# Two MLPs computed from rounded halves in three products instead of in fp32

## What is computed

```python
# layer three (L2)
h = _layer_norm(x, ln_mlp_scale, ln_mlp_offset)
h = jax.nn.gelu(h @ w_fc1 + b_fc1, approximate=False) @ w_fc2 + b_fc2
return x + h
# layer four (L3), after its two attentions
ln_out = layernorm(x, ln3_s, ln3_b)
mlp_out = gelu(ln_out @ w1 + b1) @ w2 + b2
return x + mlp_out
```

## Time and profile before

| | us |
|---|---|
| median of 3 runs | 2345.29 (2340.04 to 2346.04) |
| the profiled execution | 2333.35 |
| its span on the core | 2331.6 |
| TensorE busy | 2082.6 (89%) |
| ScalarE, VectorE, GpSimd busy | 995.9, 944.8, 658.7 |
| mean granted TensorE clock | 0.949 of full speed |
| MLPs of layer three | 1698.7 to 1849.2 |
| attention of layer four | 1849.3 to 2206.1 |
| MLPs of layer four | 2206.1 to 2326.9 |

### The profile page before, as it was taken

One profiled execution on the slowest core, in us unless ns is written; L12 is line 12 of the kernel. 1 busy time (PEld: TensorE's weight loads), 2 busy tenths in 40 slices (PEclk: granted clock), 3 DMA queues, 4 the chain that ended last, 5 costly groups with the idle time before them and its releaser, 6 DMA issues.

```text
span 2331.6 us, 37925 instructions
## 1 busy us (share of the span) xinstructions
PE 2082.6 (89%) x15565; PEld 1649.3 (71%) x15565; DVE 944.8 (41%) x1726; ACT 995.9 (43%) x2601; POOL 658.7 (28%) x768
## 2 busy tenths in 40 slices
PE   7877788887899999999899999999889877878799
PEld 4555566654688888888788888888755555666566
DVE  3433222302454444445454444444311267667510
ACT  3332344351343443434343343434344356666522
POOL 2311212112232231313223132321120156656500
PEclk9987899997999999999999999999989898989899
DMA  4000000001010000000001000000020100000000
GB/s 135 10 6 1 6 1 1 1 1 41 3 44 19 10 28 1 28 1 19 1 19 46 1 28 10 10 1 1 1 83 0 46 1 2 6 1 6 1 19 19
DMA packets 28174, 38.36 MB, mean 16 GB/s; under 512 B 1744, under 2 KB 19808, under 8 KB 28000
## 3 DMA queue, kind: packets, MB, share of 16 engines
q1 hardware_dynamic: 28000, 35.93, 4.8%
HBM read 33.83 MB, written 2.10 MB: 15 GB/s over the span
## 4 chain that ended last, share of the span: by engine, by line
PE 75%; DVE 8%; ACT 8%; issue 3%; POOL 3%; DMA 1%; SPq 0%; DVEq 0%; ACTq 0%; POOLq 0%
PE ps L184 33%; PE ps L2105 6%; PE ps_four L2251 5%; PE ps_four L2271 4%; PE ps_four L2089 4%; PE ps L2089 3%; PE ps_four L2260 2%; ACT l_pt L1472 2%; POOL l_sm L1322 2%; PE ps_four L2019 2%; PE ps L2147 2%; DVE l_sm L1829 2%; PE ps L2281 1%; PE ps L2057 1%; PE ps L2065 1%
## 5 line engine op out<-in xcount | busy, mean ns | idle before, releaser
L1566 ACT ACTIVATE l_prob<-ps_four,l_mx 128x129 f32<-128x129 f32 x512 | 181.3, 367 | 593.5 <-DVE l_mx L1864 593.5
L1356 POOL TENSOR_TENSOR l_prob<-l_prob,l_mx 128x516 f32<-128x516 f32 x128 | 134.1, 1048 | 779.5 <-DVE l_mx L1871 779.5
L184 PE MATMUL ps<-l_hT,l_wq 128*128 128x512 f32 x768 | 210.8, 410 | 6.5 <-DVE l_V L1852 6.5
L184 PE MATMUL ps<-ctxT,l_wk 128*128 128x512 f32 x768 | 214.3, 415 | 0.0
L184 PEld LDWEIGHTS ps<-l_wo,l_ao 128*128 128x128 f32 x1536 | 197.8, 188 | 21.1 <-DVE l_ao L1883 7.0
L184 PE MATMUL ps<-l_wo,l_ao 128*128 128x256 f32 x1536 | 204.9, 283 | 5.5 <-DVE l_ao L1883 5.5
L184 PE MATMUL ps<-l_wv,ctxT 128*128 128x512 f32 x768 | 204.6, 402 | 3.7 <-POOL l_wv L1294 3.4
L1322 POOL TENSOR_TENSOR l_sm<-l_sm,l_mask 128x1024 f32<-128x1024 f32 x64 | 149.9, 2363 | 155.7 <-DVE l_sm L1829 155.7
L184 PEld LDWEIGHTS ps<-l_wv,ctxT 128*128 128x128 f32 x768 | 143.8, 190 | 47.4 <-ACT l_qT L1547 9.0
L1795 DVE TENSOR_TENSOR x_tok<-x_tok,ps 128x512 f32<-128x512 f32 x100 | 64.7, 684 | 274.1 <-PE ps L2105 212.1
L184 PEld LDWEIGHTS ps<-l_hT,l_wq 128*128 128x128 f32 x768 | 135.8, 190 | 30.3 <-issue 7.2
(11 more groups left out here) (230 smaller groups left out, 3797.6 us busy)
## 6 DMA issues: line engine op xcount, KB each, us to landing
l_staging<-in_L_xattn_wv SPq DMA_DIRECT2D x8, 512.0 KB, 3.8
l_staging<-in_L_xattn_wk SPq DMA_DIRECT2D x8, 512.0 KB, 3.9
l_staging<-in_L_xattn_wq SPq DMA_DIRECT2D x8, 512.0 KB, 4.2
l_staging<-in_L_xattn_wo SPq DMA_DIRECT2D x8, 512.0 KB, 3.8
x_tok<-in_x SPq DMA_DIRECT2D x4, 512.0 KB, 7.4
ctx_tok<-in_ctx SPq DMA_DIRECT2D x4, 512.0 KB, 5.8
l_mlp_w<-in_L_xattn_mlp_w SPq DMA_DIRECT2D x2, 1024.0 KB, 8.8
l_w<-in_L_xattn_w_fc SPq DMA_DIRECT2D x2, 1024.0 KB, 6.3
```

What stands on the lines that cost most here:

```text
L184: ins = e.matmul(out, a, b, start=start and i == 0, stop=stop and i == 2, skip_group_check=not check)
L1356: e.tensor_tensor(pr[:, :, 0:S + 1], pr[:, :, 0:S + 1], mx[:, 3, :].unsqueeze(2).to_broadcast([P, GB, S + 1]), ALU.mult).then_inc(sem("poo ...
L1566: ins = e.activation(pr.t[:, b, 0:S + 1], banks[b // 2].t[:, (b % 2) * (S + 2):(b % 2) * (S + 2) + S + 1], ACT.Exp, bias=mx[:, 1, b:b + 1] ...
```

## The change

`mlp_split` takes the place of `mlp32` in both layers (layer two keeps `mlp32`):

- `w1` and `w2` are split in halves by VectorE, each in two pieces of 128 x 1024 (`mlp_w`): for layer three before and during the first MLP, for layer four behind the attention.
- The normalised input of each MLP is split by VectorE, two pieces of 128 x 512 (`mhs`), into a tile that exists once.
- Up and down are `matmul_split`: six instructions of 512 columns, and twelve of 256.
- Gelu is made twice from the bank: once into the high half of the hidden tile (rounded), once back into the bank itself in fp32. VectorE subtracts the first from the second into the low half (`hid3`). The hidden tile exists twice.
- In the code below the first `hid3` is ScalarE's, the second VectorE's, `mhs` is VectorE's and `up3` TensorE's. `down3`, `mlp_w` and `mlp_tiles` are built alike.
- The down product of chunk `k - 2` follows the up product of chunk `k` (before: `k - 1`).
- The tiles of layer four's attention (`l3_sm`, `l3_pt`, `l3_mask2`) share memory with the MLP tiles, before and after them.

```diff
+    def mlp_weights(self, phase, landed):
+        for name in ("w1", "w2"):
+            for part in range(2):
+                self.pl.emit("mlp_w", phase, name, part, landed=landed)
+                yield
+
+    def mlp_input(self, u, m, hs_done):
+        pl = self.pl
+        yield from pl.until(self.mhs)
+        pl.slot(self.mhs, "mhs", m)
+        for c in range(DC):
+            pl.emit("mhs", m, c, src=u, src_done=hs_done)
+            yield
+        pl.free(*u, by=("dve.mhs", m, DC - 1))
+
+    def mlp_split(self, m, phase, b1, func):
...
+        for k in range(FC + 2):
+            if k < FC:
+                yield from pl.until(self.misc)
+                pl.bank(self.misc, "up3", m, k)
+                pl.emit("up3", m, k)
+                yield
+            if k == FC - 1:
+                pl.free("mhs", m, by=("full", "up3", m, k))
...
+            if k >= 2:
+                pl.emit("down3", m, k - 2)
+                pl.free("hid3", m, k - 2, by=("pe.down3", m, k - 2))
+            if k < FC:
+                pl.slot(self.hid3, "hid3", m, k)
+                pl.emit("hid3", m, k)
+                pl.free("up3", m, k)
+            yield
...
         def norm3(g):
             yield from output("b", g, "w_co")
             h_done["l3e", g] = yield from normalised(3, g, "b2")
+            if g >= 2:
+                yield from self.mlp_input(("hs", ("l3n", 3, g)), ("l3e", g), h_done["l3e", g])
...
-        run(norm2(0))
-        interleave(mlp2(0), chain(norm2(1), self.load_weight("l3_w_kv", a["L3_xattn_w_kv"], "pool")), 1.2)
+            first, weights = norm2(0), self.mlp_weights("l2m", ("sp.l2m_plain", 32))
+            for stages, n in ((first, 5), (weights, 2)):
+                for _ in range(n):
+                    next(stages)
+            run(first)
+            interleave(mlp2(0), chain(weights, norm2(1), self.load_weight("l3_w_kv", a["L3_xattn_w_kv"], "pool")), 1.2)
...
-        run(rest)
+        attention.close()
+        probs_done, over_done = ("full", "four", "l3", N - 1, 1), ("full", "over", "l3", N - 1)
+        self.mlp_tiles("l3e", scope, (probs_done, over_done, ("pool.l3_scores", N - 1)))
+        interleave(rest, self.mlp_weights("l3e", ("sp.l3_mlp", 32)), 1.0)
...
+        def hid3(m, k):
+            f, bk, hid = self.mlps[m], use["up3", m, k], use["hid3", m, k]
+            q.wait_ge(*pl.event(("full", "up3", m, k)))
+            q.wait_ge(*pl.event(hid.before))
+            table(f["func"])
+            e.activation(hid.t[:, 0, :], bk.t, f["func"], bias=f["b1"][:, k:k + 1])
+            e.activation(bk.t, bk.t, f["func"], bias=f["b1"][:, k:k + 1]).then_inc(sem("act.hid3"), 1)
...
+        def mhs(m, c):
...
+            e.tensor_copy(hi, src).then_inc(sem("dve.mhs:hi"), 1)
+            q.wait_ge(*pl.done("dve.mhs:hi", m, c))
+            e.tensor_tensor(lo, src, f32(hi), ALU.subtract).then_inc(sem("dve.mhs"), 1)
+
+        def hid3(m, k):
+            bk, hid = use["up3", m, k], use["hid3", m, k].t
+            q.wait_ge(*pl.done("act.hid3", m, k))
+            e.tensor_tensor(hid[:, 1, :], bk.t, f32(hid[:, 0, :]), ALU.subtract).then_inc(bk.slot.empty, 1)
...
+        def up3(m, k):
...
+            q.wait_ge(*pl.done("dve.mlp_w", f["phase"], "w1", 1))
+            q.wait_ge(*pl.done("dve.mhs", m, DC - 1))
+            bk = fill("up3", m, k)
+            for c in range(DC):
+                ins = matmul_split(e, bk.t, [half[:, c, k * P:(k + 1) * P] for half in w], [half[:, c, :] for half in hs],
+                                   c == 0, c == DC - 1)
+            ins.then_inc(bk.slot.full, 1)
```

More of the change, by code:

```diff
@@ L196, in __init__ @@
         self.x_done, self.dma_n = [None] * G, {}
-        self.last_norm, self.slack = {}, 0
+        self.last_norm, self.slack, self.mlp_w = {}, 0, {}
     def sb(self, name, shape, dt=F32, scope=None):
@@ L644, in mlp32 @@
         pl = self.pl
-        self.mlps[m] = dict(hs=hs, hs_done=hs_done, w1=w1, w2=w2, b1=b1, func=func, landed=landed)
+        self.mlps[m] = dict(down="pe.mlp_down", hs=hs, hs_done=hs_done, w1=w1, w2=w2, b1=b1, func=func, landed=landed)
         for k in range(FC + 1):
@@ L1092, in halves, with mlp_halves @@
         return self.pl.use[src].t[:]
+    def mlp_halves(self, phase, name):
+        return [self.mlp_w[phase, name][0][:, i] for i in range(2)]
     def rows_of(self, u, b):
```

86 lines of the change are left out of this document (66 added, 20 removed).

## The result

| | median, us | range | ratio to before, 95% interval |
|---|---|---|---|
| before, beside it | 2338.90 | 2336.24 to 2346.04 (6 runs) | |
| after | 2355.40 | 2350.57 to 2360.48 (6 runs) | 1.0064 [1.0042, 1.0085] |

What follows compares the result with a forecast made beforehand. TensorE was taken as the bound, with 75% of the time. Terms of -35.2, +15.3, +6.8, +2.85, +19.9 and +2.9 summed to +12.5 us; from the runs' median of 2345.29 that gave 2358 us, range 2345 to 2374 (8 in 10).

Steps and rivals of the forecast that it cites:

- a, the products: Up and down products of the MLPs: a chunk falls from 3.44 to 2.89 us, -35.2 us over 64 chunks.
- rival of the cheap product: MLP products at half the fp32 price: 20 us less, minus 7, giving 2338 us; chance 0.04.
- b, the starts: First up products of layers three and four wait for VectorE's rounding of weights and input: +8.3 and +7.0 us.
- c, the tails: At each MLP's end the last down product waits 0.85 us for the last chunk's gelus and subtraction: eight times, +6.8 us.
- d, the seams: Between MLPs the next up product waits for the input's rounding, 0.85 us at four seams: +2.85 us in all.
- e, the transposes: TensorE's waits at the normalisations' transposes beside the MLPs grow, as two downs now stand behind them: +19.9 us, largest term.
- Rival 1: The waits at the transposes don't grow: 2338 us, or 2333 with the clock kept up too; chance 0.13.
- f, the clock: TensorE restarts at half clock after idle time: four at 1.7 us, 6.9 against 4.0 now, +2.9 us (0 to 6).
- Rival 3: VectorE is slower than its medians, all rounding at stretched durations: 2371 us; chance 0.14.

Runs made afterwards that it cites:

- starts: The kernel after, with layer three's first GpSimd bias addition held until the input's halves are made and layer four's w2 rounded later: 2343.11 us, ratio 1.0016 to before.
- three_hid: The kernel after, with a third buffer for the halves of the hidden rows in layer four's MLPs: 2349.64 us, ratio 1.0034 to before.
- transposes_late: The kernel after, with the normalisations' transposes placed later in TensorE's order in layer three's second and third MLP: 2328.22 us, ratio 0.9949 to before.
- after_again: The kernel after, unchanged, run and profiled once more: 2355.38 us, ratio 1.0075 to before.
- after_warm2: The kernel after, with unneeded TensorE products filling its long waits, made to end before the data arrive: 2338.62 us, ratio 1.0007 to before.
- two_behind_only: The kernel before, with only the order changed: down products two chunks behind up products, fp32 products and one gelu kept: 2348.44 us, ratio 1.0031 to before.
- combined_warm: The kernel after with late transposes, changed starts, third layer-four hidden buffer, filler products in three waits, one earlier input rounding: 2313.51 us, ratio 0.9890 to before.

## Why the prediction was right, and where its terms were off

Sign and size were right (+12.5 us forecast, +15, 10 to 20, measured), and the largest loss is the one it named, the waits at the transposes. But its terms were off in both directions and cancelled, and that is luck.

The time came near by luck too. 2358 us is 12 above the sum for the profiled execution, by the 2345.29 of three runs; beside the result the median of before was 2338.90, and from there the same +12.5 us give 2351.4, where 2355.4 was measured.

**a, the products: -39.7 us, not -35.2.** A chunk takes 2.82 us, not 2.89: the up product 1.38 us, not the 1.47 of the earlier trace rows, the down product 1.44 for 1.42. The rival of the cheap product (2.58 to 2.60 us) falls: a product of 512 columns with a weight load before it takes 1.38 / 6 = 230 ns. The Trainium skill ("TensorE: Matmul & The Clock Gate", Back-to-back issue gap) gives 216 ns for an isolated one and some 131 ns in a stream with weight loads; these MLPs are above both. The term was off by a reading of the earlier trace rows: the prediction took the first distance there, 1.47 us (1204.52 to 1205.99), for six products of 512 columns; the next six in the same rows take 1.39 (1205.99 to 1207.38), beside the 1.38 of after. 64 times 0.07 is 4.5 us. Its sentence that TensorE never waits in the MLPs holds for layer three's last MLP, not for all: the earlier trace rows show the waits that term e counts.

**b, the starts: 8.1 and 6.7 us, forecast 8.3 and 7.0.** Right, with its mechanism: starts took GpSimd away and the subtraction fell to 1.23 us, and took w2's copy away and the wait went.

**c, the tails: eight of 0.68 us, forecast 0.85.** The step was right (three_hid). The pair of gelus takes 0.58 + 0.65 = 1.23 us. The row that was missing is there now: 0.65 us with PSUM as the destination (fp32), 0.69 with SBUF (rounded), as for the fp32 tile of the earlier trace rows. The Trainium skill ("ScalarE: Activation LUTs", Step-by-step) calls PSUM the lower-latency one, and this trace agrees, by 0.04 us.

**d, the seams: 1.11 us twice and 0.43 twice, and 1.54 at layer three's end: 4.6 us, less the 0.85 of the earlier trace rows that went, +3.8; forecast +2.85.** Behind layer three's MLPs TensorE waited for the additions to `x_tok` that empty the side banks, which the prediction had not looked at there, not for the input's halves.

**e, the transposes: +17.8 us, forecast +19.9.** First transposes 6.41 (forecast 6.9), evacuation 0.87 (1.3), second ones 2.8 (2.7), first MLP 2.54 (3.2), layer four 2.27 and 1.77 (2.5 and 1.7): 26.7 against 8.9 us in before. That it was the largest loss, and a matter of place, is shown by transposes_late. Rival 1 falls with it.

**f, the clock: the term that was mis-sized.** Forecast +2.9: four restarts at 1.7 us, less 4.0 in before. The half-clock loss in the MLPs of before is 3.8 us, so that part was right. In after it is 13.7 us, in after_again 17.7: **+9.9 and +13.9**. Price and count failed both. The four stretches that the prediction counted cost 2.2, 3.2, 2.8 and 2.4 us, 10.6 together and not 6.9. Two more, behind the waits of 2.78 us in layer three's second MLP and of 2.27 in layer four, cost 1.5 and 1.7; after_again has the third one shown above. Behind the tails, the seams and the waits of 2.54 and 1.77 us the clock of after stayed at 1.00. after_warm2 bears the size out in time: its MLP stages are 11.4 and 15.2 us shorter than those of the two profiles. In two_behind_only the same shows at another size: 7 us more of waiting in layer three's MLPs came with 6 us more of busy TensorE (147.8 against 141.7).

The sum with the measured terms is -39.7 + 14.8 + 5.4 + 3.8 + 17.8 + 9.9 = +12.0 us by the first profile; its MLP stages are 14.3 us longer. Of the 2.3 us between them most can be the first product behind each of the 23 waits (1.69 us for 1.59); this is an estimate. The prediction came out right partly because a, c and e were too dear by 8 us and d and f too cheap by as much. Rival 3, a generally slower VectorE, did not come: copies and subtractions had the durations of the earlier trace rows except beside GpSimd.

## What to carry to other kernels

When a product gets cheaper, the work that stands in front of a dependent instruction on the same engine shrinks with it, and what was hidden there comes out: look first at what is placed beside the shortened part, and place it again (27 us here, for two lines of the plan). A wait of TensorE can cost more than its length: here 51 us of waits in the MLPs (the terms b to e) came with 14 to 18 us lost at 1.2 GHz behind them, so price both, and expect the second to differ between executions. A change that frees one wait can open another (3.57 us in combined_warm), so look at the next engine in line. A copy that waits for a late event must not stand ahead of work that is ready.
